# Gated cross-attention in fp32 on one core: probabilities transposed once per batch, their stacked rows copied by DMA inside SBUF, and the loads around the value loop reordered

## The chip, the core and the metric

The kernel runs on one core of a Trainium2 chip. The metric is the device time in microseconds (us) of the whole program.

## What is computed

With x of 16 x 512 x 512 (batch, queries, width) and a context of 16 x 77 x 512:

```
qp = x @ Wq + bq;  kp = ctx @ Wk + bk;  vp = ctx @ Wv + bv
w  = softmax(qp @ kp^T / sqrt(512))            # 512 x 77 for each batch
a  = w @ vp
gate = concat(qp, a) @ Wg + bg
out  = a * mask * sigmoid(gate) + x
```

## The kernel before, in words

Everything is fp32 in and out. Matmuls run on operands split into a high part (rounded to the matmul's own type, fp32r) and a low part (what the rounding leaves); a product is the sum of high x high, high x low and low x high.

**Set-up.** The program first makes weight products: `g`, `wqg` (the first half of the gate as a matrix applied to x), and `mt` (the keys folded with Wq and Wk). Then the value loop runs over ten tiles of 128 context rows (`k` = 0 to 9, plus one closing round). Each round transposes the values of the tile before (`turn_v`), makes the next tile's values (`v`) and the gate's share of the values (`vg`). ScalarE (ACT) writes the high parts, VectorE (DVE) or GpSimd (POOL) the low parts, and SyncE's queue (SP) stores them to `v_dram` (`store_v`, `store_vg`). Into the last rounds SP mixes the loads of batch 0: `x_raw` (x transposed, four chunks; one buffer only) and `x_rows`. ScalarE and GpSimd split `x_raw` of batch 0 into `xT` (high L478, low L731) in round 7, between the pieces of the value loop.

**Batch loop.** For each of 16 batches TensorE runs, in this written order: `gate_main` for query tile 0 (12 matmuls, L414), half of `gate_main` for tile 1, `turn_probs` (eight transposes), the other half, `attend` 0 (four matmuls: two into the gate's bank, L437 and L438, two into the attention's bank, L444 and L445), `gate_main` 2, `attend` 1, the scores of the next batch (`scores_T`, 12 matmuls), `attend` 2, `gate_main` 3 with the transposes of the next scores (`turn_scores`, L383) in its middle, `attend` 3.

**Probabilities before.** The softmax is on VectorE, its exponential on ScalarE. The result `prob` is split into high and low. Attention needs high x v_high, low x v_high and high x v_low, which is three products of 77 rows each. They are packed into two matmuls: `w_a` holds the 77 high columns and 45 of them again, `w_b` the 77 low columns and the other 32 high ones. ScalarE makes the repeated columns (`stack_probs`, L537 and L538). TensorE transposes `w_a` and `w_b` (L424, L427), and ScalarE copies both results to `wT` (L559, L561). `v_ext`, loaded from `v_dram` by four DMAs (77, 77, 45 and 32 rows of 4 KB), stacks the values' high and low rows to match.

**Queues.** SP issues its transfers in program order, waits included: in a batch `v_ext` of the next batch, then a wait for all low parts of the next `xT` (`xT_lo`), `x_raw` of the batch after it, then four output stores, each followed by a load of `x_rows`. ScalarE's first `tanh` of the batch loop waits until every value store has landed, since its buffer lies where the stores read from.

Of the kernel before, what the change touches and what calls it, by code (L numbers as in the profile page):

```python
# [27 lines left out]
LO_A = 45  # L28
LO_B = S - LO_A
K_A, K_B = S + LO_A, S + LO_B  # L30
# [44 lines left out]
def build(nc, io):  # L75
    with ExitStack() as es:
# [29 lines left out]
        w_a = sb("w_a", D0 + 6272, [P, T, K_A])  # L106
        w_b = sb("w_b", D0 + 6784, [P, T, K_B])
# [38 lines left out]
        prob = shifted  # L146
# [56 lines left out]
        def _(sync):  # L203
# [71 lines left out]
            for k in range(KT):  # L275
# [3 lines left out]
                if k == 5:  # L279
                    sync.wait_ge(dots_made, DOT["sb", 3] + 1)  # L280
                    load_xT(0, (0, 1))
                if k == 6:
                    load_xT(0, (2, 3))
                if k == 7:
# [3 lines left out]
                if k == 8:  # L288
# [29 lines left out]
        def _(pe):  # L318
# [57 lines left out]
            def turn_scores(b):  # L376
# [3 lines left out]
                else:  # L380
                    pe.wait_ge(wTb_made, b)
# [35 lines left out]
            def turn_probs(b):  # L417
                pe.wait_ge(prob_split, b + 1)
                pe.wait_ge(stacked_a, b + 1)
                pe.wait_ge(stacked_b, b + 1)  # L420
                if b == 0:
                    pe.wait_ge(job_drained, last_in_bank(7))
                for t in range(T):
                    last = pe.transpose(turn_ps[0:K_A, t * P:(t + 1) * P], w_a[:, t, :], ident[:, :])  # L424
                last.then_inc(wa_turned, 1)
                for t in range(T):
                    last = pe.transpose(score_ps[0:K_B, t * P:(t + 1) * P], w_b[:, t, :], ident[:, :])  # L427
                last.then_inc(wb_turned, 1)

            def attend(b, t):  # L430
                n, q, v = b * T + t, slice(t * P, (t + 1) * P), v_ext[b % 2]
                if t == 0:
                    pe.wait_ge(wTa_made, b + 1)
                    pe.wait_ge(wTb_made, b + 1)
                    pe.wait_ge(vext_in[b % 2], 64 * (b // 2 + 1))
                ps = gate_ps[n % 3]
                pe.matmul(ps[:, :], wT[0:K_A, 0, q], v[0:K_A, 0, D:2 * D], start=False, stop=False)  # L437
# [6 lines left out]
                pe.matmul(ps[:, :], wT[0:K_A, 0, q], v[0:K_A, 0, 0:D], start=True, stop=False)  # L444
# [22 lines left out]
        def _(act):  # L467
# [67 lines left out]
            def stack_probs(b):  # L535
                act.wait_ge(prob_hi, b + 1)
                act.activation(w_a[:, :, S:K_A], w_a[:, :, 0:LO_A], ACT.Copy).then_inc(stacked_a, 1)  # L537
                act.activation(w_b[:, :, S:K_B], w_a[:, :, LO_A:S], ACT.Copy).then_inc(stacked_b, 1)  # L538
# [256 lines left out]
```

## Time and profile before

| what | value |
|---|---|
| time, median of 3 runs | 432.78 us (431.98 to 433.77) |
| time of the profiled execution | 434.12 us |
| its span | 432.3 us |
| TensorE busy | 417.7 us (97%) |
| VectorE, ScalarE, GpSimd busy | 215.5, 151.9, 126.8 us |
| mean granted TensorE clock | 0.992 of full |
| DMA | 90.86 MB, mean 210 GB/s |

A busy TensorE is not one at its peak: its matmuls are pipelined and each row's duration holds the overlap with its neighbours, so lengths of stretches are read from start times. In the chain of work the durations run from one step to the next and add up to the span.

### The profile page before, as it was taken

To read this page: it belongs to the slowest core of one execution; us is meant where nothing else is said; L and a number is where in the kernel's file an instruction comes from. 1 tells how busy PE (TensorE), PEld (TensorE's weight loads), DVE (VectorE), ACT (ScalarE), POOL (GpSimd) and SP (SyncE) were. 2 spreads that over 40 slices of the span, in tenths; PEclk is the share of its full clock that TensorE was granted. 3 is DMA by queue.
4 is the path that set the end of the run, shared out by engine and by line. 5 is a ranking of instruction groups with operands and counts; after the bars stand their busy time and mean duration, and the time that the engine had idled before them with its cause. 6 is when DMAs were issued, how large, how long until landed. Compare 5 with 4: busy or idle time off the path is not lost.

```text
span 432.3 us, 5334 instructions
## 1 busy us (share of the span) xinstructions
PE 417.7 (97%) x1940; PEld 335.3 (78%) x1940; DVE 215.5 (50%) x385; ACT 151.9 (35%) x283; POOL 126.8 (29%) x98
## 2 busy tenths in 40 slices
PE   8999999998996999999999999999999999999996
PEld 4879978886774787787877878787787878778784
DVE  4786546553450646354463634546253553725453
ACT  5644243224222243241423324143342424324131
POOL 0004154346524051340505225050432505143100
PEclk9999999999898999999999999999999999999999
DMA  8975434457589766957577595766758567685312
GB/s 271 389 276 213 143 83 192 155 205 226 195 243 265 249 182 228 291 158 259 187 229 237 182 278 167 240 199 231 226 198 277 162 230 211 216 253 194 119 49 97
DMA packets 43125, 90.86 MB, mean 210 GB/s; under 512 B 5276, under 2 KB 5276, under 8 KB 42460
## 3 DMA queue, kind: packets, MB, share of 16 engines
q1 hardware_dynamic: 42524, 89.48, 63.5%
q10 hardware_dynamic: 576, 1.05, 0.6%
q8 instruction: 15, 0.25, 0.2%
q14 instruction: 10, 0.08, 0.1%
HBM read 63.51 MB, written 27.00 MB: 209 GB/s over the span
## 4 chain that ended last, share of the span: by engine, by line
PE 90%; DMA 5%; DVE 2%; ACT 1%; POOL 1%; SPq 1%; issue 0%; DVEq 0%; ACTq 0%
PE bank L414 40%; PE bank L322 31%; PE bank L437 4%; PE bank L438 4%; PE bank L444 3%; PE bank L445 3%; DMA v_ext<-v_dram 2%; PE bank L424 2%; PE bank L427 2%; DMA x_raw<-in_xT 1%; DMA wqT_raw<-in_wqT 1%; PE bank L383 1%; PE bank L365 1%; DMA v_dram<-v_st 1%; POOL v_st L731 1%
## 5 line engine op out<-in xcount | busy, mean ns | idle before, releaser
L414 PE MATMUL bank<-wqg,xT 128*128 128x512 f32 x768 | 191.8, 396 | 0.0
L414 PEld LDWEIGHTS bank<-wqg,xT 128*128 128x128 f32 x768 | 142.8, 189 | 29.4
L731 POOL TENSOR_TENSOR xT<-x_raw,xT 128x512 fp32r<-128x512 f32 x64 | 87.9, 1403 | 191.3 <-ACT xT L478 191.3
L695 DVE SCALAR_TENSOR_TENSOR prod_sb<-tanh_sb,bank 128x512 f32<-128x512 f32 x64 | 43.9, 686 | 123.1 <-ACT tanh_sb L550 123.1
L550 ACT ACTIVATE tanh_sb<-bank 128x512 f32<-128x512 f32 x64 | 38.4, 599 | 129.3 <-PE bank L438 121.7
L706 DVE SCALAR_TENSOR_TENSOR out_sb<-prod_sb,half_mask,x_rows 128x512 f32<-128x512 f32 x64 | 49.1, 768 | 1.7
L322 PE MATMUL bank<-xT,mt 128*77 128x512 f32 x192 | 47.1, 394 | 0.0
L322 PEld LDWEIGHTS bank<-xT,mt 128*77 128x77 f32 x192 | 28.0, 146 | 15.7
L478 ACT ACTIVATE xT<-x_raw 128x512 fp32r<-128x512 f32 x64 | 35.2, 617 | 3.2 <-DMA x_raw<-in_xT 3.2
L322 PE MATMUL bank<-wg,vT 128*128 128x512 f32 (+1 forms) x120 | 30.7, 407 | 2.6 <-DVE vT L577 2.6
L322 PE MATMUL bank<-wv,ctxT 128*128 128x512 f32 (+1 forms) x120 | 30.2, 401 | 0.0
L322 PEld LDWEIGHTS bank<-wg,vT 128*128 128x128 f32 (+1 forms) x120 | 23.3, 195 | 8.7 <-DVE vT L577 3.0
L437 PE MATMUL bank<-v_ext,wT 122*128 122x512 f32 x64 | 25.7, 402 | 4.2 <-DMA v_ext<-v_dram 4.2
L322 PE MATMUL bank<-ctxT,g_s 128*128 128x416 f32 x144 | 27.4, 352 | 0.6 <-DVE ctxT L573 0.6
L322 PEld LDWEIGHTS bank<-ctxT,g_s 128*128 128x128 f32 x144 | 26.8, 188 | 1.3 <-DVE ctxT L573 1.0
L444 PE MATMUL bank<-v_ext,wT 122*128 122x512 f32 x64 | 25.8, 403 | 0.0
L438 PE MATMUL bank<-v_ext,wT 109*128 109x512 f32 x64 | 25.7, 402 | 0.0
L445 PE MATMUL bank<-v_ext,wT 109*128 109x512 f32 x64 | 25.7, 402 | 0.0
L322 PEld LDWEIGHTS bank<-wv,ctxT 128*128 128x128 f32 (+1 forms) x120 | 21.7, 186 | 4.6
L533 ACT ACTIVATE expd<-shifted 128x308 f32<-128x308 f32 x16 | 7.4, 462 | 38.6 <-DVE shifted L675 38.6
L592 DVE TENSOR_SCALAR sT<-bank,sb_c 77x512 f32<-77x512 f32 x16 | 12.0, 747 | 17.8 <-PE bank L322 17.8
L731 POOL TENSOR_TENSOR v_st<-vg_f,v_st 128x512 fp32r<-128x512 f32 (+1 forms) x10 | 13.4, 1338 | 16.5 <-ACT v_st L469 16.5
(75 smaller groups left out, 378.7 us busy)
## 6 DMA issues: line engine op xcount, KB each, us to landing
x_raw<-in_xT SPq DMA_DIRECT2D x64, 256.0 KB, 5.2
x_rows<-in_x SPq DMA_DIRECT2D x64, 256.0 KB, 3.7
out_y<-out_sb SPq DMA_DIRECT2D x64, 256.0 KB, 2.0
v_ext<-v_dram SPq DMA_DIRECT2D x32, 308.0 KB
v_dram<-v_st SPq DMA_DIRECT2D x18, 512.0 KB, 3.2
v_ext<-v_dram SPq DMA_DIRECT2D x16, 180.0 KB
ctxT_raw<-in_ctxT SPq DMA_DIRECT2D x4, 624.0 KB, 10.7
ctx_rows<-in_ctx SPq DMA_DIRECT2D x4, 616.0 KB
```

The lines of the kernel that those rows point to most:

```text
L322: last = pe.matmul(ps, lhs(s, c), rhs(m, c), start=(c == 0 and n == 0), stop=(c == C - 1 and n == 2))
L414: pe.matmul(gate_ps[n % 3][:, :], xT[b % 2][:, s, c, q], wqg[:, m, c, :], start=(c == 0 and (s, m) == PRODUCTS[0]), stop=False)
L437: pe.matmul(ps[:, :], wT[0:K_A, 0, q], v[0:K_A, 0, D:2 * D], start=False, stop=False)
L438: pe.matmul(ps[:, :], wT[0:K_B, 1, q], v[0:K_B, 1, D:2 * D], start=False, stop=True).then_inc(gate_done, 1)
L444: pe.matmul(ps[:, :], wT[0:K_A, 0, q], v[0:K_A, 0, 0:D], start=True, stop=False)
L445: pe.matmul(ps[:, :], wT[0:K_B, 1, q], v[0:K_B, 1, 0:D], start=False, stop=True).then_inc(attn_done, 1)
L478: act.activation(xT[b % 2][:, HI, c], x_raw[:, c], ACT.Copy).then_inc(xT_hi, 1)
L550: act.activation(tanh_sb[:, n % 2, :], gate_ps[n % 3][:, :], ACT.Tanh, scale=0.5).then_inc(tanh_made, 1)
L592: dve.tensor_scalar(sT[:, :], sT_ps[0:S, :], sb_c[:, b:b + 1], None, ALU.add).then_inc(sT_made, 1)
L695: dve.scalar_tensor_tensor(prod_sb[:, n % 2, :], tanh_sb[:, n % 2, :], 1.0, attn_ps[n % 2][:, :], ALU.add, ALU.mult).then_inc(prod_made, 1)
L706: dve.scalar_tensor_tensor(out_sb[:, t, :], prod_sb[:, n % 2, :], half_mask[:, n:n + 1], x_rows[b % 2][:, t, :], ALU.mult, ALU.add).then_i ...
L731: pool.tensor_tensor(dst, src, f32(hi_), ALU.subtract).then_inc(made, 1)
```

## The change

The probabilities are no longer split before the transposes. VectorE writes them in fp32 with 19 of the 77 columns repeated (96 in all). TensorE transposes them once (four transposes in place of eight), ScalarE copies the 96 rows to `wT` as the high part, VectorE subtracts this from the transposed fp32 values to give the low part (`low_probs`), and two DMAs issued by ScalarE copy 2 x 32 high rows to partitions 96 to 127 of `wT`'s two halves. The transposes stand after the first `gate_main`; all of the second stands behind them. `attend` 0 waits for both copies and for the low part. `v_ext` takes five loads, one of them of 19 rows. The split of the next batch's `xT` by ScalarE follows the copy to `wT` and the two DMA issues. In the value loop the loads of `x_raw` and `x_rows` for batch 0 are issued one round earlier, and `v_ext` of batch 0 goes ahead of `x_raw` of batch 1.

```diff
-LO_A = 45
-LO_B = S - LO_A
-K_A, K_B = S + LO_A, S + LO_B
+Q = 32
+TOP = 3 * Q
+DUP = S - (TOP - S)
+K_B = TOP + DUP - Q
...
-                sync.dma_start(f32(v_ext[i][S:K_A, 0, :]), v_dram[r:r + LO_A, LO, :]).then_inc(vext_in[i], 16)
-                sync.dma_start(f32(v_ext[i][S:K_B, 1, :]), v_dram[r + LO_A:r + S, LO, :]).then_inc(vext_in[i], 16)
+                sync.dma_start(f32(v_ext[i][S:TOP, 0, :]), v_dram[r + DUP:r + S, LO, :]).then_inc(vext_in[i], 16)
+                sync.dma_start(f32(v_ext[i][TOP:P, 0, :]), v_dram[r:r + Q, LO, :]).then_inc(vext_in[i], 16)
+                sync.dma_start(f32(v_ext[i][S:K_B, 1, :]), v_dram[r + DUP - (K_B - S):r + DUP, LO, :]).then_inc(vext_in[i], 16)
...
-                if k == 5:
+                if k == 4:
                     sync.wait_ge(dots_made, DOT["sb", 3] + 1)
                     load_xT(0, (0, 1))
+                if k == 5:
+                    load_xT(0, (2, 3))
...
-            sync.wait_ge(xT_lo, C)
-            load_xT(1)
             sync.wait_ge(job_done, J["v", KT - 1] + 1)
             wait_stored(2)
             load_vext(0)
+            sync.wait_ge(xT_lo, C)
+            load_xT(1)
             load_vext(1)
...
-                    pe.wait_ge(wTb_made, b)
+                    pe.wait_ge(shift_made, b)
...
-                pe.wait_ge(prob_split, b + 1)
-                pe.wait_ge(stacked_a, b + 1)
-                pe.wait_ge(stacked_b, b + 1)
+                pe.wait_ge(prob_made, b + 1)
+                pe.wait_ge(prob_twice, b + 1)
...
-                    last = pe.transpose(turn_ps[0:K_A, t * P:(t + 1) * P], w_a[:, t, :], ident[:, :])
-                last.then_inc(wa_turned, 1)
-                for t in range(T):
-                    last = pe.transpose(score_ps[0:K_B, t * P:(t + 1) * P], w_b[:, t, :], ident[:, :])
-                last.then_inc(wb_turned, 1)
+                    last = pe.transpose(turn_ps[0:TOP, t * P:(t + 1) * P], prob[:, t, :], ident[:, :])
+                last.then_inc(turned, 1)
...
-                    pe.wait_ge(wTa_made, b + 1)
-                    pe.wait_ge(wTb_made, b + 1)
-                    pe.wait_ge(vext_in[b % 2], 64 * (b // 2 + 1))
+                    pe.wait_ge(wT_dup, 32 * (b + 1))
+                    pe.wait_ge(wT_lo, b + 1)
+                    pe.wait_ge(vext_in[b % 2], 80 * (b // 2 + 1))
...
+            def high_probs(b):
+                act.wait_ge(turned, b + 1)
...
+                act.activation(wT[0:TOP, 0, :], turn_ps[0:TOP, :], ACT.Copy).then_inc(wT_top, 1)
+                act.wait_ge(wT_top, b + 1)
+                act.dma_start(f32(wT[TOP:P, 0, :]), f32(wT[0:Q, 0, :])).then_inc(wT_dup, 16)
+                act.dma_start(f32(wT[TOP:P, 1, :]), f32(wT[Q:2 * Q, 0, :])).then_inc(wT_dup, 16)
...
-                stack_probs(b)
+                high_probs(b)
                 if more:
                     xT_hi_of(b + 1)
-                act.wait_ge(wa_turned, b + 1)
-                act.activation(wT[0:K_A, 0, :], turn_ps[0:K_A, :], ACT.Copy).then_inc(wTa_made, 1)
-                act.wait_ge(wb_turned, b + 1)
-                act.activation(wT[0:K_B, 1, :], score_ps[0:K_B, :], ACT.Copy).then_inc(wTb_made, 1)
...
+            def low_probs(b):
+                dve.wait_ge(wT_top, b + 1)
+                dve.tensor_tensor(wT[0:S, 1, :], turn_ps[0:S, :], f32(wT[0:S, 0, :]), ALU.subtract).then_inc(wT_lo, 1)
```

TensorE at the start of a batch, before the change. L414 is `gate_main`, L424 and L427 are the transposes, L437 to L445 are `attend`; `wqg`, `xT` and `wT` are named above.

```order
L414 MATMUL bank<-wqg,xT_69 128x512 x18
L424 MATMUL bank<-ident,w_a 122x128 x4
L427 MATMUL bank<-ident,w_b 109x128 x4
L414 MATMUL bank<-wqg,xT_69 128x512 x6
L437 MATMUL bank<-v_ext_60,wT 128x512
```

The same place after the change, where the lines have moved by one or two:

```order
L415 MATMUL bank<-wqg,xT_68 128x512 x12
L426 MATMUL bank<-ident,prob 96x128 x4
L415 MATMUL bank<-wqg,xT_68 128x512 x12
L436 MATMUL bank<-v_ext_60,wT 128x512
```

Four transposes are gone, the others stand six matmuls earlier, and twelve matmuls in place of six lie between them and `attend`.

ScalarE in one batch, before: the two stacking copies, the high parts of the next `xT`, the two copies to `wT`, the tanhs.

```order
L537 ACTIVATE w_a<-w_a 128x4x45
L538 ACTIVATE w_b<-w_a 128x4x32
L478 ACTIVATE xT_70<-x_raw 128x512 x4
L559 ACTIVATE wT<-bank 122x512
L561 ACTIVATE wT<-bank 109x512
L550 ACTIVATE tanh_sb<-bank 128x512 x3
```

And after:

```order
L539 ACTIVATE wT<-bank 96x512
L541 DMA wT<-wT 32x512
L542 DMA wT<-wT 32x512
L476 ACTIVATE xT_69<-x_raw 128x512 x4
L554 ACTIVATE tanh_sb<-bank 128x512 x3
```

The copy to `wT` and two DMA issues now stand ahead of the `xT` split, which stood ahead of the copies to `wT`.

SP at the end of the value loop, before (L261 is `store_vg`, L256 `store_v`, L251 the loads of `x_raw`, L265 to L268 those of `v_ext`; the last L261 is the last value store):

```order
L256 DMA v_dram<-v_st_75 192x1x512
L261 DMA v_dram<-v_st_74 256x1x512
L251 DMA x_raw<-in_xT 128x512 x4
L265 DMA v_ext_60<-v_dram 77x1024
L266 DMA v_ext_60<-v_dram 77x1024
L267 DMA v_ext_60<-v_dram 45x1024
L268 DMA v_ext_60<-v_dram 32x1024
L265 DMA v_ext_61<-v_dram 77x1024
```

And after, down to the last value store:

```order
L265 DMA v_ext_60<-v_dram 77x1024
L266 DMA v_ext_60<-v_dram 77x1024
L267 DMA v_ext_60<-v_dram 19x1024
L268 DMA v_ext_60<-v_dram 32x1024
L269 DMA v_ext_60<-v_dram 45x1024
L251 DMA x_raw<-in_xT 128x512 x4
L265 DMA v_ext_61<-v_dram 77x1024
L266 DMA v_ext_61<-v_dram 77x1024
L267 DMA v_ext_61<-v_dram 19x1024
L268 DMA v_ext_61<-v_dram 32x1024
L269 DMA v_ext_61<-v_dram 45x1024
L261 DMA v_dram<-v_st_74 192x1x512
```

`v_ext` of batch 0 now goes first, with a load of 19 rows in it, and `x_raw` of batch 1 stands between the two `v_ext`.

## Rows read from the trace of the kernel before

**Rows 1.** The page: engines' busy time, and shares of the chain that ended last.

```profile
PE 417.7 (97%) x1940; PEld 335.3 (78%) x1940; DVE 215.5 (50%) x385; ACT 151.9 (35%) x283; POOL 126.8 (29%) x98
PE 90%; DMA 5%; DVE 2%; ACT 1%; POOL 1%; SPq 1%; issue 0%; DVEq 0%; ACTq 0%
```

**Rows 2.** TensorE's waits: releaser, total us, times, longest us.

```profile
PE bank L437 <- DMA v_ext<-v_dram: 4.2, 1, 4.2
PE bank L322 <- DVE vT L577: 2.6, 1, 2.6
```

**Rows 3.** The chain in order of time: start us, length us, step.

```profile
85.43 5.53 PE bank L322 x24
91.39 5.54 PE bank L322 x24
101.01 5.19 DMA x_raw<-in_xT
108.73 4.57 PE bank L322 x12
113.74 5.54 PE bank L322 x24
...
126.70 9.58 DMA v_ext<-v_dram
138.47 3.40 PE bank L414 x12
```

**Rows 4.** The chain in the batch that starts at 225 us.

```profile
225.39 4.10 PE bank L414 x18
229.48 0.44 PE bank L424 x4
...
232.69 2.74 PE bank L414 x12
...
236.37 2.79 PE bank L322 x12
```

**Rows 5.** Timeline of that batch: start us, length us, engine, instruction, idle before.

```profile
226.69 2.18 ACT L478 ACTIVATE xT<-x_raw 128x512 fp32r<-128x512 f32 x4
227.39 5.57 POOL L731 TENSOR_TENSOR xT<-x_raw,xT 128x512 fp32r<-128x512 f32 x4 [13.12 <-ACT xT L478]
228.98 0.41 SPq L265 DMA_DIRECT2D v_ext<-v_dram  x1
229.32 0.60 PE L424 MATMUL bank<-ident,w_a 128*122 128x128 f32 x4
229.96 0.60 ACT L559 ACTIVATE wT<-bank 122x512 fp32r<-122x512 f32 x1 [1.08 <-PE bank L424]
```

**Rows 6.** Windows: busy us, then granted clock, DMA share, GB/s at the end.

```profile
229.00:229.50 0.50, 0.50 (x5) 0.37 (x4) 0.00 (x0) 0.00 (x0) 0.50 (x2) 1.00 1.00 389
231.50:232.00 0.50, 0.50 (x4) 0.42 (x3) 0.00 (x0) 0.00 (x0) 0.50 (x2) 1.00 0.68 246
...
136.40:140.00 3.60, 3.58 (x9) 2.88 (x10) 0.00 (x0) 0.00 (x0) 0.00 (x0) 0.54 0.76 261
```

**Rows 7.** Issue time (ns, min/median/max) and landing: wkT_raw's (two rows), out_y's.

```profile
L481 ACTq DMA_DIRECT2D wkT_raw<-in_wkT x4: 404/456/627, 0.7 to 2.1; - x4
DMA to landing us min/median/max: 3.6/5.6/7.7
...
DMA to landing us min/median/max: 2.0/2.0/6.8
```

**Rows 8.** Timeline of batch 0.

```profile
129.63 0.60 SPq L261 DMA_DIRECT2D v_dram<-v_st  x1
140.59 0.60 ACT L550 ACTIVATE tanh_sb<-bank 128x512 f32<-128x512 f32 x1 [7.56 <-DMA v_dram<-v_st]
141.23 0.69 DVE L695 SCALAR_TENSOR_TENSOR prod_sb<-tanh_sb,bank 128x512 f32<-128x512 f32 x1 [11.76 <-ACT tanh_sb L550]
147.74 0.43 PE L383 MATMUL bank<-ident,sT 77*128 77x77 f32 x4
```

More of the change, by code:

```diff
@@ L105, in build @@
         expd = sb("expd", D0 + 5952, [P, T, S])
[L106 to L107 removed]
+        prob = sb("prob", D0 + 6272, [P, T, TOP])
         wv = sb("wv", E0, [P, 2, C, D], F32R)
@@ L417, in turn_probs @@
             def turn_probs(b):
[L418 to L420 removed]
+                pe.wait_ge(prob_made, b + 1)
+                pe.wait_ge(prob_twice, b + 1)
                 if b == 0:
                     pe.wait_ge(job_drained, last_in_bank(7))
+                else:
+                    pe.wait_ge(wT_lo, b)
                 for t in range(T):
[L424 to L428 removed]
+                    last = pe.transpose(turn_ps[0:TOP, t * P:(t + 1) * P], prob[:, t, :], ident[:, :])
+                last.then_inc(turned, 1)
             def attend(b, t):
@@ L432, in attend @@
                 if t == 0:
-                    pe.wait_ge(wTa_made, b + 1)
-                    pe.wait_ge(wTb_made, b + 1)
-                    pe.wait_ge(vext_in[b % 2], 64 * (b // 2 + 1))
+                    pe.wait_ge(wT_dup, 32 * (b + 1))
+                    pe.wait_ge(wT_lo, b + 1)
+                    pe.wait_ge(vext_in[b % 2], 80 * (b // 2 + 1))
                 ps = gate_ps[n % 3]
-                pe.matmul(ps[:, :], wT[0:K_A, 0, q], v[0:K_A, 0, D:2 * D], start=False, stop=False)
+                pe.matmul(ps[:, :], wT[:, 0, q], v[:, 0, D:2 * D], start=False, stop=False)
                 pe.matmul(ps[:, :], wT[0:K_B, 1, q], v[0:K_B, 1, D:2 * D], start=False, stop=True).then_inc(gate_done, 1)
@@ L443, in attend @@
                 ps = attn_ps[n % 2]
-                pe.matmul(ps[:, :], wT[0:K_A, 0, q], v[0:K_A, 0, 0:D], start=True, stop=False)
+                pe.matmul(ps[:, :], wT[:, 0, q], v[:, 0, 0:D], start=True, stop=False)
                 pe.matmul(ps[:, :], wT[0:K_B, 1, q], v[0:K_B, 1, 0:D], start=False, stop=True).then_inc(attn_done, 1)
@@ L450, in _ @@
                 gate_main(b, 0)
-                gate_main(b, 1, range(0, C // 2))
                 turn_probs(b)
-                gate_main(b, 1, range(C // 2, C))
+                gate_main(b, 1)
                 attend(b, 0)
@@ L533, in exps @@
                 act.activation(expd[:, :, :], shifted[:, :, :], ACT.Exp, scale=SCALE).then_inc(exp_made, 1)
[L535 to L538, printed above, removed]
+            def high_probs(b):
+                act.wait_ge(turned, b + 1)
+                if b == 0:
+                    act.wait_ge(wT_zeroed, 1)
+                else:
+                    act.wait_ge(attn_done, b * T)
+                act.activation(wT[0:TOP, 0, :], turn_ps[0:TOP, :], ACT.Copy).then_inc(wT_top, 1)
+                act.wait_ge(wT_top, b + 1)
+                act.dma_start(f32(wT[TOP:P, 0, :]), f32(wT[0:Q, 0, :])).then_inc(wT_dup, 16)
+                act.dma_start(f32(wT[TOP:P, 1, :]), f32(wT[Q:2 * Q, 0, :])).then_inc(wT_dup, 16)
             def tanh_tile(b, t):
@@ L707, in output @@
                                          x_rows[b % 2][:, t, :], ALU.mult, ALU.add).then_inc(out_made, 1)
+            dve.wait_ge(job_done, J["v", KT - 1] + 1)
+            dve.memset(f32(wT[2 * Q:TOP, 1, :]), 0.0).then_inc(wT_zeroed, 1)
             softmax_max(0)
             softmax_rest(0)
+            dve.wait_ge(wT_zeroed, 1)
             for b in range(B):
                 more = b + 1 < B
+                low_probs(b)
                 product(b, 0)
```

19 lines of the change are left out of this document (7 added, 12 removed).

## The prediction

> **What bounds the kernel now.** I read the page first: TensorE is busy 97% of the span, and 90% of the chain that ended last is TensorE [rows 1]. So in a batch only two things count: TensorE's own instructions, and any wait newly put in front of them. The list of TensorE's waits shows where it does not run: once 4.2 us for `v_ext` and once 2.6 us for `vT` [rows 2]. In the 15 batches behind the first it waits for nothing. The chain in order of time then says what these two waits cost in all. Rounds of the value loop start every 5.96 us (85.43, 91.39); three rounds after 91.39 would be 109.27, and the chain has that start at 113.74, so the wait behind the late `x_raw` (a step of 5.19 us from 101.01) costs 4.47 us, not 2.6. The rest is clock: the 12 matmuls behind the wait take 4.57 us [rows 3] where 12 like them take 2.79 [rows 4]. The same shows behind the 4.2 us wait, where the granted clock is 0.54 (near 1.2 GHz in place of 2.4 [rows 6]) and 12 gate matmuls take 3.40 us [rows 3] against 2.74 [rows 4]. Last I read the timeline of one batch for the distances between transposes, copies and the `xT` split [rows 5], and of batch 0 for what stands behind its wait [rows 8].
>
> **1. The earlier `x_raw` of batch 0.** ScalarE waits in round 7 for chunks that SP issued only just before, and the transposed values queue behind it. One round earlier is 5.96 us earlier, more than the 5.19 us of the transfer. The wait and its slow clock go: -4.47 us. ScalarE still does four more high parts in that round and GpSimd four low ones, so the next piece may be late by some tenths: I take -4.2, with -3.0 and -4.5 as bounds.
>
> **2. The start of batch 0.** `v_ext` of batch 0 no longer stands behind 1 MB of `x_raw`. Its transfer took 9.58 us from 126.70 [rows 3]; issued some 2.5 us earlier and ahead of that megabyte, it should cease to hold TensorE: -4.2, and about -1.6 more by the clock. But what is late next? ScalarE's first tanh began at 140.59, released by the last value store, which was issued at 129.63 [rows 8]. That store stays behind both `v_ext` and `x_raw`, so the tanh is not earlier relative to the loop. `attend` 2 needs its product (0.69 us [rows 8]) and the next transposes of scores (147.74 before) need VectorE behind two products and two outputs, which I put at 144.9 if the store lands as now. So this part gives at most -2.9, not -5.8.
> The store can also be later. Between 231.5 and 232 us, when only the 77-row loads of `v_ext` are moving, the DMA share is 0.68 at 246 GB/s, against 1.00 at 389 when 128-row transfers move [rows 6]: 0.68 is 11 of 16 engines, 22 GB/s each, and 77 is 7 x 11. If a load's rows are dealt only in equal parts, 19 rows (78 KB) go to one engine: 3.5 us for each of the two `v_ext` ahead of the store, +7 us if nothing else is waited for, and then the tanh costs +4 instead. I take the middle, a store later by 2.5 us: -0.5 in all, bounds -2.9 and +4.
> The page "DMA: Bandwidth & Descriptors" of the Trainium skill (section "Why a DMA increments its semaphore by 16 and not by 1") says that a DMA uses the largest number of engines up to 16 that divides the slowest dimension: 11 for 77 rows, 1 for 19. The trace agrees for the 77.
> Within later batches the 19 rows cost nothing: `v_ext` is issued at 228.98 [rows 5] for an `attend` a whole batch (18.7 us) later.
>
> **3. Four transposes fewer.** Each group of four takes 0.44 us of the chain [rows 4]. 15 batches x -0.44 = -6.6 us (batch 0's is hidden in part 2). ScalarE's stacking and VectorE's split lie beside TensorE's work and are worth nothing. The low part, new on VectorE (77 x 512 out of PSUM, as long as a product, 0.69), runs beside the DMA copies and ends before them. The probabilities are wanted six matmuls (1.4 us) earlier, and VectorE saves two steps ahead of that; only in batch 0 is TensorE likely to wait (about 0.9 us, inside part 2).
>
> **4. The new wait, the copies.** Count from the first transpose (T). ScalarE's copy begins at T+0.64 and takes 0.60 (229.96 against 229.32 [rows 5]), so the first copy's DMA can be issued at T+1.29. An issue on ScalarE takes at least 0.40 us [rows 7], so the second starts at T+1.69. TensorE has 0.44 of transposes and 2.74 of gate matmuls [rows 4], and loads the weights of `attend` about 0.2 earlier: it wants `wT` at T+2.99. What is not in the trace is the landing of a 64 KB copy inside SBUF. Nearest rows: `out_y`, 256 KB, lands at best 2.0 us after its issue; `wkT_raw`, also on ScalarE's queue and beside SP's loads, at best 3.6 [rows 7]. Less the time of the 192 KB more that `out_y` moves (0.5 us at 389 GB/s), the lower bound is 1.5: landed T+3.19, a wait of 0.2. At 3.6 the wait is 2.3. I take 2.0, smaller than `out_y` but in the midst of the `v_ext` and `x_rows` traffic: landed T+3.69, a wait of 0.7 us per batch, nearer the lower row since size and target are nearer to it. 15 x 0.7 = +10.5. The gap should be too short for the clock to fall.
>
> **5. The `xT` split.** It moves behind the copy and both issues. ScalarE starts it at T+2.1; GpSimd follows 0.70 later and takes 5.57 [rows 5]: done at T+8.4. TensorE, without part 4's wait, wants it for the next scores at T + 0.44 + 2.74 + 0.94 + 3.68 = T+7.8 (0.94 is `attend`: 3.68 from 232.69 to 236.37 less 2.74 [rows 4]). So even with instant copies it would wait some 0.56 us in 14 batches. Behind a wait of 0.7 this is covered and adds nothing, but it is a floor: at most 0.14 of part 4 could be won back by faster copies. SP's `x_raw` moves later by as much and has 12 us to spare.
>
> **Sum:** -4.2 - 0.5 - 6.6 + 10.5 = -0.8 us. On the profiled span that is 432.3 to 431.5. The profiled execution took 434.12, 1.8 more than its span and 1.3 above the median, and on the median of 432.78 the forecast is 432.0: no change. A measurement can tell about 0.5% (2.2 us) from none.
>
> **Rivals.**
> (a) Faster: the copies land in 1.5 us and the last value store as now. Then part 5's floor decides: 14 x 0.56 + 0.2 = +8.0, part 2 gives -2.9: -4.2 - 2.9 - 6.6 + 8.0 = -5.7, so 427.1. If the issues are shorter or GpSimd takes 4 x 1.3 alone, 424. For it: no wait at all today and light traffic at that moment in parts of a batch; against it: the 1.00 DMA share at 229 us [rows 6], just where the copies will run. Chance 0.32.
> (b) Slower: the copies queue behind the `v_ext` packets on each engine. At a landing of 2.7 the wait is 1.4, 15 x 1.4 = +21, sum +9.7: 442.5. It decides from a wait of 0.9 (a landing of 2.2) upward; at 3.6 the time would be 456. For it: the same busy share, and two queues that shared the engines at the start landed in 3.6 or later. Chance 0.28.
> The section "Queues, rings and completion order" of the same page of the Trainium skill says that an engine takes whole packets of many descriptors from one queue before it turns to the next; each `v_ext` load gives an engine seven rows of 4 KB, and behind those a copy would be late by about 1 us each. No row here shows it.
> (c) Slower by the first batch: the 19-row loads keep one engine behind, the first tanh is late by 6 us or more, part 2 is +4 and the clock falls once more (+1.8): 438. Chance 0.06.
> (d) The reorder does nothing, since the value loop waits for GpSimd's split instead: part 1 is 0, 436. Chance 0.03.
>
> **How the numbers follow.** The forecast (within 0.5%, 430.6 to 434.9) has 0.31. Range 426 to 443: it takes in (a)'s main value and (b)'s, and leaves out (a)'s 424 and (b)'s tail, together 2 in 10. The forecast's own range is 430 to 435. Faster 0.33 is (a) and the forecast's edge; slower 0.35 is (b), (c) and half of (d); same 0.32.
>
> **What would show it.** Part 1: no TensorE wait for `vT` near 106 us, and the batch loop starting some 4 us earlier, near 121. Part 2: no wait for `v_ext`, a wait for a product or for `sT` in batch 0. Part 3: one group of four transposes, 0.44 us. Part 4: 15 waits of `attend` 0 for DMA `wT`, 0.7 us each. Part 5: waits of the scores for GpSimd near zero. The prediction is wrong if the landing of the copies is not about 2.0 us, or if the clock falls behind each wait.

## The result, and the profile after

The changed kernel takes 550.59 us (median of 4 runs, 546.04 to 552.31) beside 433.27 us (431.98 to 434.62) for the kernel before on the same chip: 1.269 times as long, with a 95% interval of 1.260 to 1.278. The forecast was 432.0 with a range of 426 to 443.

The page after, busy time and the shares of the chain that ended last, to be held against [rows 1]:

```profile
PE 443.5 (82%) x1876; PEld 347.8 (64%) x1876; DVE 216.2 (40%) x386; ACT 136.7 (25%) x235; POOL 118.1 (22%) x98
PE 65%; DMA 23%; ACT 3%; DVE 2%; SPq 2%; POOL 2%; issue 2%; ACTq 1%; DVEq 0%
```

TensorE has 64 instructions fewer, as the change says, and yet is busy 26 us longer: each matmul takes longer on average, which is a slower clock (the profiled execution has a granted clock of 0.912 in the mean, before 0.992). And DMA, 5% of the chain before, is 23%. The list of TensorE's waits (total us, times, longest) names the transfer:

```profile
PE bank L436 <- DMA wT<-wT: 89.9, 16, 7.0
PE bank L426 <- DVE prob L685: 1.4, 1, 1.4
...
PE bank L323 <- DVE vT L577: 0.9, 1, 0.9
```

Sixteen waits for the copies of 64 KB inside SBUF. Fifteen of them are 6.0 us long in the mean ((89.9 - 0.5) / 15). The last batch loads no `v_ext` for a batch behind it, and there the second copy takes 2.00 us and the wait is 0.5 us. A row of the chain and one of TensorE's timeline:

```profile
528.01 2.00 DMA wT<-wT
```

```profile
530.06 0.50 PE L436 MATMUL bank<-v_ext,wT 128*128 128x512 f32 x1 [0.51 <-DMA wT<-wT]
```

The wait for `vT` fell from 2.6 to 0.9 and that for `v_ext` is gone [rows 2]. There is none for GpSimd's `xT`.

The chain after, in the batch that answers to [rows 4] (start us, length us, step):

```profile
233.59 0.45 PE bank L426 x4
...
234.06 0.60 ACT wT L539
...
234.69 0.54 ACTq L541
...
235.26 7.16 DMA wT<-wT
...
242.47 0.79 PE bank L436
243.26 0.43 PE bank L437
...
244.54 4.25 PE bank L415 x12
...
257.44 2.78 PE bank L415 x12
```

One group of four transposes is left, 0.45 us. Then come ScalarE's copy, the first issue, and 7.16 us of the second copy's transfer, under which TensorE's twelve gate matmuls lie. Behind the wait three of the four matmuls of `attend` take 0.43 us each (0.23 at 249 us), and the twelve gate matmuls 4.25 us (2.78 a little later, at 257.44): the clock is down. Between 155.94 and 501.48 us this chain has 14 steps `DMA wT<-wT`, one in each batch that loads `v_ext`, so a batch takes (501.48 - 155.94) / 13 = 26.6 us in place of 18.7.

The timeline of that batch, beside [rows 5]:

```profile
233.43 0.60 PE L426 MATMUL bank<-ident,prob 128*96 128x128 f32 x4
233.69 0.41 SPq L265 DMA_DIRECT2D v_ext<-v_dram  x1
234.06 0.60 ACT L539 ACTIVATE wT<-bank 96x512 fp32r<-96x512 f32 x1 [3.09 <-PE bank L426]
...
234.69 0.54 ACTq L541 DMA_DIRECT2D wT<-wT  x1
...
235.19 0.42 SPq L269 DMA_DIRECT2D v_ext<-v_dram  x1
235.26 0.61 ACTq L542 DMA_DIRECT2D wT<-wT  x1
242.47 0.79 PE L436 MATMUL bank<-v_ext,wT 128*128 128x512 f32 x1 [5.69 <-DMA wT<-wT]
```

SP issues its five loads of `v_ext`, nearly 1 MB, from 0.26 us behind the first transpose on. Both copies are issued in the midst of them, and they land last. The issues are nearly where the prediction put them (T+1.26 and T+1.83, T being 233.43, where it had T+1.29 and T+1.69). What is far off is the landing, the time from the issue until the last piece has arrived. The transfers issued in 0.1 us from 234.68 and from 235.25 (KB each, us from issue to landing) give it for either copy:

```profile
wT<-wT ACTq DMA_DIRECT2D x1, 64.0 KB, 5.8
...
wT<-wT ACTq DMA_DIRECT2D x1, 64.0 KB, 7.2
```

What moved meanwhile shows in the packets of the two queues (q1 is SP's, q10 ScalarE's; packets, MB, share of 16 engines) in 236.5 to 237.5, 237.5 to 239 and 239 to 240.5 us:

```profile
q1 hardware_dynamic: 47, 0.14, 53.4%
q10 hardware_dynamic: 22, 0.03, 8.7%
...
q1 hardware_dynamic: 99, 0.34, 65.3%
q10 hardware_dynamic: 10, 0.01, 2.2%
...
q1 hardware_dynamic: 65, 0.18, 43.2%
q10 hardware_dynamic: 50, 0.07, 16.0%
```

For 1.5 us the engines carry 99 packets of `v_ext` and 10 of the copies, then 50 of the copies in as long a time. The last 13 packets of the copies go in the 2 us behind these windows. The windows of that time (us, busy of PE, PEld, DVE, ACT and POOL, then clock, DMA share, GB/s) say what is still moving, and what TensorE gets:

```profile
237.50:238.50 1.00, 0.00 (x0) 0.00 (x0) 0.00 (x0) 0.61 (x2) 1.00 (x2) 1.00 0.67 223
...
240.50:242.50 2.00, 0.03 (x1) 0.03 (x1) 0.00 (x0) 0.00 (x0) 1.05 (x1) 0.58 0.10 35
...
241.50:242.00 0.50, 0.00 (x0) 0.00 (x0) 0.00 (x0) 0.00 (x0) 0.06 (x1) 0.50 0.06 25
...
243.00:247.50 4.50, 4.50 (x12) 3.47 (x11) 1.44 (x2) 0.60 (x1) 0.00 (x0) 0.50 0.81 270
```

First a share of 0.67, which is 11 of 16 engines as in [rows 6]. In the last two microseconds it is 0.10, and 0.06, one engine of 16, from 241.5 to 242 us. These rows don't name the load that is still moving. That it is the one of 19 rows fits e1 below, where these rows are split: there such a share (0.10) lasts only from 239.0 to 239.5 us ahead of the second copy's landing at 239.9. The granted clock, 1.00 while TensorE first stands, is 0.58 there and 0.50 (1.2 GHz in place of 2.4) in the 4.5 us behind the wait, though TensorE is busy all through them.

Batch 0, the timeline beside [rows 8]:

```profile
121.60 2.97 PE L415 MATMUL bank<-wqg,xT 128*128 128x512 f32 x12
126.00 0.61 PE L426 MATMUL bank<-ident,prob 128*96 128x128 f32 x4 [1.43 <-DVE prob L685]
128.39 0.59 SPq L261 DMA_DIRECT2D v_dram<-v_st  x1
135.73 0.79 PE L436 MATMUL bank<-v_ext,wT 128*128 128x512 f32 x1 [6.35 <-DMA wT<-wT]
144.49 1.09 ACT L554 ACTIVATE tanh_sb<-bank 128x512 f32<-128x512 f32 x2 [6.71 <-DMA v_dram<-v_st]
148.69 0.48 PE L384 MATMUL bank<-ident,sT 77*128 77x77 f32 x4
```

The batch loop starts at 121.60, 3.6 us earlier than before (125.21 there). At the next transposes of scores, 148.69 against 147.74, this and more is gone again.

**Where the time went.** The spans differ by 111.7 us. The waits for the copies are 89.9 of it. The loop's start gives -3.6, the transposes 16 x -0.44 = -7.0, the lost `v_ext` wait -4.2, the wait for `prob` +1.4. What is left, 111.7 - 89.9 + 3.6 + 7.0 + 4.2 - 1.4 = 35.2 us, is 2.3 us for each of the 15 long waits. That fits the slow clock. In the batch shown it is 4.25 - 2.77 for twelve gate matmuls and 2.08 - 0.94 for `attend`, 2.6 us together. Over the 14 batches of the chain the twelve matmuls behind the wait take 3.2 to 4.7 us, 3.96 in the mean, and with `attend` that is 2.3 us more than at full clock.

### The profile page after: what moved, and what is told of

The parts are those of the page before. It is cut to its first block, busy times and chain, and to the rows that moved or that the text cites. A ratio compares the mean times of both kernels' runs of the same rounds, so it can differ in the third digit from the quotient of the medians.

```text
span 544.0 us, 5238 instructions
## 1 busy us (share of the span) xinstructions
PE 443.5 (82%) x1876; PEld 347.8 (64%) x1876; DVE 216.2 (40%) x386; ACT 136.7 (25%) x235; POOL 118.1 (22%) x98
## 4 chain that ended last, share of the span: by engine, by line
PE 65%; DMA 23%; ACT 3%; DVE 2%; SPq 2%; POOL 2%; issue 2%; ACTq 1%; DVEq 0%
PE bank L415 26%; PE bank L323 23%; DMA wT<-wT 19%; PE bank L436 4%; PE bank L437 3%; PE bank L444 3%; PE bank L443 3%; DMA v_dram<-v_st 3%; ACT wT L539 2%; ACTq L541 1%; PE bank L426 1%; POOL xT L738 1%; PE bank L384 1%; DMA wkT_raw<-in_wkT 1%; POOL v_st L738 1%
## 5 line engine op out<-in xcount | busy, mean ns | idle before, releaser
L415 PE MATMUL bank<-wqg,xT 128*128 128x512 f32 x768 | 211.4, 425 | 0.0
L415 PEld LDWEIGHTS bank<-wqg,xT 128*128 128x128 f32 x768 | 158.4, 210 | 36.7
L738 POOL TENSOR_TENSOR xT<-x_raw,xT 128x512 fp32r<-128x512 f32 x64 | 79.5, 1273 | 309.3 <-ACT xT L476 309.3
L436 PE MATMUL bank<-v_ext,wT 128*128 128x512 f32 x64 | 31.2, 488 | 89.9 <-DMA wT<-wT 89.9
L436 PEld LDWEIGHTS bank<-v_ext,wT 128*128 128x128 f32 x64 | 13.5, 211 | 99.3 <-DMA wT<-wT 96.7
L323 PE MATMUL bank<-wg,vT 128*128 128x512 f32 (+1 forms) x120 | 29.1, 391 | 0.9 <-DVE vT L577 0.9
L444 PE MATMUL bank<-v_ext,wT 122*128 122x512 f32 x64 | 28.9, 452 | 0.0
L443 PE MATMUL bank<-v_ext,wT 128*128 128x512 f32 x64 | 28.9, 452 | 0.0
L437 PE MATMUL bank<-v_ext,wT 122*128 122x512 f32 x64 | 28.8, 450 | 0.0
L323 PEld LDWEIGHTS bank<-wg,vT 128*128 128x128 f32 (+1 forms) x120 | 22.1, 185 | 6.5 <-DVE vT L577 1.3
L690 DVE TENSOR_TENSOR wT<-bank,wT 77x512 fp32r<-77x512 f32 x16 | 11.0, 687 | 29.8 <-ACT wT L539 29.8
L539 ACT ACTIVATE wT<-bank 96x512 fp32r<-96x512 f32 x16 | 9.5, 596 | 48.3 <-PE bank L426 48.3
```

Source lines behind the costliest of these rows:

```text
L323: last = pe.matmul(ps, lhs(s, c), rhs(m, c), start=(c == 0 and n == 0), stop=(c == C - 1 and n == 2))
L415: pe.matmul(gate_ps[n % 3][:, :], xT[b % 2][:, s, c, q], wqg[:, m, c, :], start=(c == 0 and (s, m) == PRODUCTS[0]), stop=False)
L436: pe.matmul(ps[:, :], wT[:, 0, q], v[:, 0, D:2 * D], start=False, stop=False)
L437: pe.matmul(ps[:, :], wT[0:K_B, 1, q], v[0:K_B, 1, D:2 * D], start=False, stop=True).then_inc(gate_done, 1)
L443: pe.matmul(ps[:, :], wT[:, 0, q], v[:, 0, 0:D], start=True, stop=False)
L444: pe.matmul(ps[:, :], wT[0:K_B, 1, q], v[0:K_B, 1, 0:D], start=False, stop=True).then_inc(attn_done, 1)
```

## The experiments

Three theories stood at the start. A: the copies queue behind the loads of `v_ext` on each DMA engine (the prediction's rival (b)). B: a copy inside SBUF from ScalarE's queue takes that long by itself. C: the load of 19 rows, all on one engine, holds up the pieces of the copies there. All kernels start from the changed one unless said otherwise. The table sums them up; "wait" is TensorE's in total for the copies, and "landing" the median over both copies of all 16 batches.

| kernel | time, us | ratio to before (95%) | wait, us | landing, us |
|---|---|---|---|---|
| changed kernel | 550.59 | 1.269 (1.260 to 1.278) | 89.9 | 6.7 |
| e1_split19 | 539.47 | 1.244 (1.235 to 1.252) | 83.8 | 6.3 |
| e2_late_vext | 450.60 | 1.039 (1.033 to 1.046) | 23.9 | 2.4 |
| e3_engine_rows | 443.74 | 1.023 (1.016 to 1.030) | none | none |
| e4_reorder_only | 431.30 | 0.994 (0.991 to 0.997) | none | none |
| e5_vext_with_copies | 543.92 | 1.246 (1.237 to 1.256) | 85.2 | 5.2 |
| e6_one_load_early | 459.69 | 1.057 (1.052 to 1.063) | 30.9 | 2.9 |
| e7_xT_first | 423.14 | 0.973 (0.968 to 0.977) | none | none |
| e8_xraw_earlier_only | 431.28 | 0.992 (0.989 to 0.994) | none | none |
| e9_together_split19 | 523.77 | 1.205 (1.197 to 1.213) | 72.6 | 4.8 |
| e10_small_shares | 472.07 | 1.086 (1.079 to 1.094) | 39.2 | 3.6 |
| e11_xT_first_19rows | 428.86 | 0.987 (0.982 to 0.993) | none | none |
| e12_dma_late_xT_first | 440.10 | 1.015 (1.008 to 1.022) | 14.2 | 2.2 |

The kernel before had medians of 433.82, 434.61 and 434.49 us beside the first, second and third four.

### e1_split19: the 19 rows as 16 and 3

```diff
-                sync.dma_start(f32(v_ext[i][S:TOP, 0, :]), v_dram[r + DUP:r + S, LO, :]).then_inc(vext_in[i], 16)
+                sync.dma_start(f32(v_ext[i][S:S + 16, 0, :]), v_dram[r + DUP:r + DUP + 16, LO, :]).then_inc(vext_in[i], 16)
+                sync.dma_start(f32(v_ext[i][S + 16:TOP, 0, :]), v_dram[r + DUP + 16:r + S, LO, :]).then_inc(vext_in[i], 16)
...
-                    pe.wait_ge(vext_in[b % 2], 80 * (b // 2 + 1))
+                    pe.wait_ge(vext_in[b % 2], 96 * (b // 2 + 1))
```

> The changed kernel with the 19-row load of v_ext issued as two, of 16 and of 3 rows; all else the same. In the changed kernel the two wT copies land 7.0 us after their issue, and in the last 1.5 us before that only one DMA engine is busy (share 0.06 to 0.08). Theory A (the copies wait on each engine for the v_ext rows that SP queued ahead of them, the engine that has all 19 rows being the last): the tail of one engine goes, landing near 5 us, the wait of attend 0 falls from 5.6 to about 3.5 us, the kernel from 550 to some 505 to 515 us. Theory B (a copy inside SBUF takes some 7 us whatever else moves): no change, 550 us. Theory C (the 19 rows on one engine are the whole cause): landing 2 to 2.5 us, about 440 us.

539.47 us. The waits are 6.1 us less in all (83.8 against 89.9), the time 11. The copies land in 6.3 us in place of 6.7. The 19-row load is not what holds them, and C falls as the main cause. A is not hit either: more is left than it said.

### e2_late_vext: the loads of `v_ext` behind the first `attend`

```diff
-                    sync.wait_ge(attn_done, b * T)
+                    sync.wait_ge(attn_done, b * T + 1)
                     load_vext(b + 1)
```

> The changed kernel with v_ext of the next batch issued after attend 0 of the running batch in place of before it, so that only an x_rows load is near the copies. Theory A: the copies land in 2 to 2.5 us, the wait of attend 0 is under 1 us in all batches but the first, the clock stays up, about 435 to 445 us. Theory B: landing stays near 7 us, about 550 us. Theory C: as A, since the 19-row load is moved too.

One constant takes 100 us off: 450.60. Here are the two copies of the batch at 232 us, each from a view of what is issued in 0.1 us or less (KB, us to landing), and then the windows from 235 us (columns as above):

```profile
wT<-wT ACTq DMA_DIRECT2D x1, 64.0 KB, 2.3
...
wT<-wT ACTq DMA_DIRECT2D x1, 64.0 KB, 3.2
```

```profile
235.00:236.50 1.50, 0.00 (x0) 0.00 (x0) 0.00 (x0) 1.11 (x3) 1.50 (x2) 1.00 0.05 18
236.50:239.00 2.50, 2.49 (x11) 2.05 (x12) 1.05 (x2) 0.60 (x1) 2.50 (x3) 1.00 0.07 16
```

The same copies with the same issues land in 2.4 us (median). So B falls: without the loads a copy is quick, as the last batch of the changed kernel already said. What made it slow is the loads of `v_ext` beside it. And behind a gap of 1.5 us the granted clock stays at 1.00. Of the 23.9 us of waits 6.2 is batch 0, where the loads are where they were; the other 15 wait 1.2 us each in the mean, from 0.5 to 2.0, and behind none of them does the clock fall.

### e3_engine_rows: the copies by ScalarE itself

```diff
-                act.dma_start(f32(wT[TOP:P, 0, :]), f32(wT[0:Q, 0, :])).then_inc(wT_dup, 16)
-                act.dma_start(f32(wT[TOP:P, 1, :]), f32(wT[Q:2 * Q, 0, :])).then_inc(wT_dup, 16)
+                act.activation(wT[TOP:P, 0, :], f32(wT[0:Q, 0, :]), ACT.Copy).then_inc(wT_dup, 1)
+                act.activation(wT[TOP:P, 1, :], f32(wT[Q:2 * Q, 0, :]), ACT.Copy).then_inc(wT_dup, 1)
```

TensorE waits for `2 * (b + 1)` of them, and ahead of the transposes for those of the batch before.

> The changed kernel with the 2 x 32 rows copied inside SBUF by two ScalarE activations (0.6 us each) in place of two DMAs. By all theories the wait for a DMA goes. ScalarE is then done at T+2.4 (T is the first transpose), before TensorE wants wT at T+3.0; the xT split starts at T+2.4 and GpSimd ends near T+8.4, so the scores wait about 0.5 us in 14 batches. Sum against the kernel before: -3.6 for the earlier batch loop, +1 to +4 for the later first tanh, -7.0 for 64 transposes, +7 for the scores' wait: 430 to 436 us. If instead something else of the change costs the time, it stays well above 440.

443.74 us, above what was expected. TensorE's waits, and below them ScalarE's first copy among the instructions on `wT` (ns, min/median/max):

```profile
PE bank L323 <- POOL xT L739: 13.3, 15, 1.8
...
PE bank L437 <- DMA v_ext<-v_dram: 2.3, 1, 2.3
```

```profile
L542 ACT ACTIVATE wT<-wT x16: 628/628/630, 127.3 to 425.7; 32x512 fp32r<-32x512 f32 x16
```

Each copy takes ScalarE 0.63 us, about what an issue of the DMA took (0.54 and 0.61), and it is finished then. No wait for `wT` is left. In its place stands the one that the prediction's part 5 had as a floor: the scores wait for GpSimd's `xT`, 1.8 us in batch 0 and 0.82 us in each of 14 others (0.56 was worked out), since the split stands behind the copies on ScalarE.

### e4_reorder_only: the kernel before with both reorders of loads

The edit is the two hunks of the change on `k == 5` to `k == 8` and on `load_xT(1)`, alone, in the kernel before.

> The kernel before with the reordered loads alone: x_raw and x_rows of batch 0 a round earlier, v_ext of batch 0 ahead of x_raw of batch 1. The probabilities and the four v_ext loads (77, 77, 45, 32 rows) are as before. Expected: the wait for vT falls from 2.6 to 0.9 us and the batch loop starts 3.6 us earlier; without 19-row loads the first tanh starts no later than before (140.6), and the v_ext wait of 4.2 us goes. 425 to 429 us. If the later first tanh (144.5 in the changed kernel) came from the order of the loads and not from the 19 rows, it shows here too and the time is 429 to 432.

431.30 us, a gain of 2.5 and less than expected. A row from its waits and one from its timeline:

```profile
PE bank L437 <- ACT wT L559: 4.5, 1, 4.5
```

```profile
137.11 0.60 ACT L550 ACTIVATE tanh_sb<-bank 128x512 f32<-128x512 f32 x1 [3.94 <-DMA v_dram<-v_st]
```

The `vT` wait is down to 0.9 us as in the changed kernel. `v_ext` is in time now, but `attend` waits 4.5 us for ScalarE's `wT`: this copy stands in order behind the split of `x_raw` of batch 1, which `v_ext` has pushed back. One wait took the place of the other. And the first tanh is at 137.11, where the changed kernel, with the same reorders and the 19-row loads, has it at 144.49.

### e5_vext_with_copies: loads and copies issued together

Since C and B had fallen and A had the size wrong, the question was what the engines do when both queues have work. If they served in the order of arrival (A1), it should help to release the loads not ahead of the copies but with them:

```diff
-                    sync.wait_ge(attn_done, b * T)
+                    sync.wait_ge(wT_top, b + 1)
                     load_vext(b + 1)
```

> The changed kernel with the five v_ext loads released by the copy to wT (the same event that releases the wT copies) in place of some 1 us before it, so that both queues are filled together. Runs so far: v_ext issued first, landing 6.7 us in the median; v_ext after attend 0, 2.4 us; 19 rows split, 6.3 us. Theory A1 (an engine takes work of both queues in order of arrival): only the v_ext load or two issued by then stand ahead, landing 3 to 4.5 us, kernel 465 to 500 us. Theory A2 (the engines favour SP's queue, or take turns with many rows at a time, as long as SP's has work): landing stays at 6 to 7 us, 535 to 555 us.

543.92 us: next to nothing. The two copies of the batch at 235 us, as for e2:

```profile
wT<-wT ACTq DMA_DIRECT2D x1, 64.0 KB, 3.4
...
wT<-wT ACTq DMA_DIRECT2D x1, 64.0 KB, 7.3
```

The first lands 2.4 us sooner than in the changed kernel, but the second, issued 0.5 us later, when only two loads had been issued, lands as late as behind all five. By the order of arrival it would stand behind two loads, 14 rows on an engine or 2.6 us at 22 GB/s [rows 6]. This run alone leaves one way out: if the load of 19 rows, issued 0.2 us behind the copy, got ahead of it, one engine would have 33 rows to move, some 6 us. e9 below closes it: with these rows split the second copies still take 6.3 us in the median of the 14 batches. So it is not the order of arrival, and A1 falls.

### e6_one_load_early: one of the five loads ahead of the copies

```diff
                     sync.wait_ge(attn_done, b * T)
-                    load_vext(b + 1)
+                    load_vext_first(b + 1)
+                    sync.wait_ge(attn_done, b * T + 1)
+                    load_vext(b + 1, False)
```

`load_vext_first` is the load of line 265 (77 rows), and the other call the four others.

> A dose: the changed kernel with one 77-row load of v_ext (308 KB on 11 engines) issued ahead of the copies as now, the other four after attend 0. If the copies wait for what is queued ahead of them, the landing lies between 2.4 us (none ahead) and 6.7 us (all ahead), by about the 1.2 us that 28 KB take on an engine: 3.5 to 4 us, kernel 465 to 485 us. If a small amount of traffic is enough to hold them, it stays above 5 us and 510 us.

459.69 us, waits of 30.9 us. In the 14 batches that load `v_ext` the mean wait is 1.22 us in e2, 1.68 here and 5.93 in the changed kernel. So one load of 77 rows ahead costs 0.5 us a batch and all five cost 4.7: ten times as much for three times the bytes. Behind two of these 14 waits, all of 1.4 to 1.9 us, the granted clock did fall (0.50 near 200 and 364 us), and these batches took 22.0 and 22.1 us where the others took 20.0 to 20.5.

### e7_xT_first: ScalarE's copies, with the split of `xT` ahead

e3 and e1 together, and in ScalarE's batch:

```diff
+                if more and b:
+                    xT_hi_of(b + 1)
                 high_probs(b)
-                if more:
+                if more and not b:
                     xT_hi_of(b + 1)
```

> The run with ScalarE copies in place of the DMAs took 443.7 us, with the scores waiting for GpSimd's xT split 15 times, 0.88 us each. Here ScalarE's high parts of the next xT are moved ahead of the copy to wT (from batch 1 on) and the 19-row load is issued as 16 and 3 rows. The split then starts 2 us earlier and ends before the scores want it; ScalarE is free again at T-0.3, before the transposes are done. Expected: no wait in batches 1 to 15, a batch of 18.3 us in place of 18.7: 443.7 - 13 for the waits - 2 for the first tanh = 426 to 430 us. If the order of ScalarE is not what costs the 0.88 us, it stays near 443.

423.14 us: 2.7% faster than the kernel before (0.968 to 0.977), and a little better than expected. Its waits in the batch loop are all in batch 0, 4.0 us together. The two longest:

```profile
PE bank L428 <- DVE prob L689: 1.4, 1, 1.4
PE bank L445 <- DVE prod_sb L702: 1.2, 1, 1.2
```

Of the 11.5 us that it gains, 3.3 are the earlier `x_raw` (e8 below). The 14 middle batches take 18.33 us in place of 18.71, together 5.3 us, which fits the four transposes fewer. The rest is in batch 0.

### e8_xraw_earlier_only: the kernel before with the first reorder alone

The edit is the hunk on `k == 5` to `k == 8`.

> The kernel before with x_raw and x_rows of batch 0 a round earlier and nothing else (v_ext of batch 0 stays behind x_raw of batch 1). The run with both reorders took 431.3 against 433.8 us. If the earlier x_raw is what gains, this one begins its batch loop 3.6 us earlier as well and keeps the 4.2 us wait for v_ext: 429 to 431 us. If both reorders were needed, 433 us.

431.28 us, a gain of 3.3. The wait for `v_ext` is still 4.2 us. So the first reorder gives all of e4's gain, and `v_ext` ahead of `x_raw` adds nothing to the kernel before that these runs can tell.

### e9_together_split19 and e10_small_shares: by what pieces do the engines take turns?

Two readings were left. T: an engine turns to the other queue only when it is through with a load's whole share of rows on it (7 of 4 KB for a 77-row load, 19 for the other), so a copy, which has pieces on all 16 engines, waits for shares of that size. S: SP's queue goes ahead as long as it has any work. e9 is e5 and e1 together. e10 leaves the time of the loads as it was and cuts them into shares of 1 to 3 rows:

```diff
-                sync.dma_start(f32(v_ext[i][0:S, 0, :]), v_dram[r:r + S, HI, :]).then_inc(vext_in[i], 16)
-                sync.dma_start(f32(v_ext[i][0:S, 1, :]), v_dram[r:r + S, HI, :]).then_inc(vext_in[i], 16)
...
+                for s in range(2):
+                    for p0, p1 in ((0, 32), (32, 64), (64, S)):
+                        sync.dma_start(f32(v_ext[i][p0:p1, s, :]), v_dram[r + p0:r + p1, HI, :]).then_inc(vext_in[i], 16)
+                for p0, p1 in ((S, S + 16), (S + 16, TOP)):
+                    sync.dma_start(f32(v_ext[i][p0:p1, 0, :]), v_dram[r + DUP + p0 - S:r + DUP + p1 - S, LO, :]).then_inc(vext_in[i], 16)
```

> Both queues filled together, as in the run where the copy to wT releases v_ext, and the 19-row load issued as 16 and 3 rows. In that run the first copy landed 3.4 us after its issue and the second 7.3, with 543.9 us. Theory T (an engine changes queue only after a DMA's whole share, so a copy waits for at most one share each time, and the second copy's last part waited for the 19-row share): no share is over 28 KB now, the second copy lands near 5 us, 490 to 515 us. Theory S (the engines serve SP's queue first while it has work): the second copy stays at 6.5 to 7.3 us, 530 to 545 us.

> The changed kernel with the same bytes of v_ext in the same place, but each 77-row load issued as 32, 32 and 13 rows and the 19 rows as 16 and 3: ten loads, and no engine has more than 3 rows (12 KB) of one, where it had 7 or 19. Theory T: a copy waits for shares of 8 to 12 KB, the second lands in 3 to 4 us, 455 to 480 us. Theory S: as much work of SP's is still there, landing 5 to 7 us, 510 to 545 us.

e9: 523.77 us, between the two, with copies at 3.3 and 6.4 us. e10: 472.07 us. The same megabyte, started at the same place, costs 78 us less. Its copies in the batch at 238 us:

```profile
wT<-wT ACTq DMA_DIRECT2D x1, 64.0 KB, 3.4
...
wT<-wT ACTq DMA_DIRECT2D x1, 64.0 KB, 3.8
```

S falls: from 241.0 to 242.5 us the engines move 91 packets of the copies beside 111 of `v_ext`. That the size of the shares matters is what T said, but e10 doesn't show it alone: ten issues take SP longer (the first six, 2.85 us), so that fewer of the loads are ahead of the copies. And e9's second copy is later than T allows. That the copies wait for `v_ext` on the engines is shown. The exact rule by which an engine changes queues stays open.

### e11_xT_first_19rows and e12_dma_late_xT_first: what each part is worth

e11 is e7 with the 19-row load as in the change. e12 is e7 with DMAs for the copies again, but with the loads of `v_ext` behind the first `attend` as in e2.

> The run of 423.1 us (ScalarE copies, xT split first, 19 rows issued as 16 and 3) without the last: the 19-row load as one. If the order on ScalarE is what took 443.7 to 423.1, the batches are 18.3 us long here too and only batch 0 is longer, by a first tanh some 4 to 7 us later of which 3 to 6 us reach TensorE: 426 to 429 us. If the split of the 19 rows counted in every batch, it is near 440.

> The changed kernel with its two wT copies by DMA, but with all that the runs showed to be in their way moved: v_ext after attend 0, xT split ahead of the copy to wT, 19 rows as 16 and 3. The copies should land in about 2.4 to 3.2 us, attend 0 waits about 1.2 us a batch. Against the 450.6 us with v_ext late alone: GpSimd's split no longer follows, the first batch gains some 4 us: 438 to 445 us, still slower than the kernel before and some 17 us behind the version with ScalarE copies. If it came below 430 the DMA itself would be no loss.

e11: 428.86 us. So the load of 19 rows costs 5.7 us (428.86 - 423.14), and the place of the split 14.9 (443.74 - 428.86). The first is all in batch 0, where `attend` waits for `v_ext`:

```profile
PE bank L437 <- DMA v_ext<-v_dram: 3.2, 1, 3.2
```

e12: 440.10 us, 5.6 us above the kernel before. Even with no `v_ext` load in their way but in batch 0, the version with DMA copies is 17 us slower than e7, the one with ScalarE's own. Its 14 middle batches take 0.8 us more each (19.14 against 18.33), and 5.2 us of its waits are in batch 0:

```profile
PE bank L437 <- DMA wT<-wT: 14.2, 16, 5.2
```

## Why the prediction was wrong

**The step that failed is in part 4**: "I take 2.0, smaller than `out_y` but in the midst of the `v_ext` and `x_rows` traffic", with an upper bound of 3.6. The copies landed 5.8 and 7.2 us behind their issues in the batch shown, 6.7 in the median. The time 2.0 was right for a copy without the loads beside it: 1.9 and 2.0 in the last batch of the changed kernel, a median of 2.2 in e12. Then the rest of the arithmetic holds too: e12's fifteen later waits are (14.2 - 5.2) / 15 = 0.6 us, where 0.7 was forecast. What was wrong is the choice "nearer the lower row since size and target are nearer to it". What decides is not what is copied but what else is queued, and [rows 7] had the row for this: `wkT_raw`, on ScalarE's queue beside SP's loads, took 3.6/5.6/7.7. Its minimum was taken as a bound, where its median and maximum were the case at hand. [Rows 5] had the other half: `v_ext` is issued 0.34 us ahead of the transposes, so nearly 1 MB starts just before the copies in 14 of the 16 batches. At the 22 GB/s of one engine [rows 6] the two times 7 rows of 4 KB on each of 11 engines are an estimated 2.6 us alone. That would have turned the forecast, though the copies were later still, by 4.3 us in the median (6.7 against 2.4 in e2). What makes up the rest is not shown.

**"The gap should be too short for the clock to fall"** followed from the 0.7 and fell with it. Behind the wait shown the clock was 0.50, and the slow stretches cost some 2.3 us for each of 15 long waits: 35 us that the sum had at zero. At e12's gaps of 0.5 to 0.7 us it didn't fall, so the sentence was right for the wait that it spoke of.

**Rival (b)** had the mechanism, and e2 shows it: queueing behind `v_ext`, with a chance of 0.28 and a price of 442.5 us, at most 456. Its price stopped at the same wrong bound. The sentence beside it drew on the Trainium skill, page "DMA: Bandwidth & Descriptors", section "Queues, rings and completion order": an engine drains a whole packet, typically 9 to 17 descriptors, from one queue before it turns to another. The trace agrees in its direction: 99 packets of `v_ext` to 10 of the copies for 1.5 us, then 50 of the copies. It doesn't show the size of a turn. By the prediction's "late by about 1 us each", the two loads of 77 rows would have given a landing of some 4 us and a wait of 2.7. This was there, but not carried into the price, and it too would have been short of the 6.7 measured.

**Part 1**, the earlier `x_raw`: -4.2 forecast. The loop starts 3.6 us earlier, and e8 is 3.3 us faster. Right, inside its bounds.

**Part 2**, the start of batch 0: -0.5 forecast, bounds -2.9 and +4. The reorder is worth nothing or slightly less than nothing (e4 against e8). The 19 rows on one engine are real: a DMA share of 0.10 at the end of the copies' wait, and 5.7 us in e11 against e7. With them the first tanh comes at 144.49, that is 22.9 us behind the start of the batch loop, where it was 15.4 before (140.59 [rows 8] less 125.21): 7.5 us later, as the upper bound supposed with its +7. The next transposes of scores are 4.6 us later by the same measure (27.1 against 22.5), where that bound had +4; but this holds batch 0's wait for the copies too. The same page of the Trainium skill, in its section "Why a DMA increments its semaphore by 16 and not by 1", gives a rule by which 19 rows go to one engine, and the share of 0.06 in the changed kernel's trace agrees. But the next thing late behind the old wait was not named: in e4 it is ScalarE's `wT`, stuck behind the split of batch 1.

**Part 3**, the transposes: 0.44 us a batch forecast, 0.45 of the chain left for the one group that stays. The middle batches of e7 and e11, in which TensorE waits for nothing, are 0.38 us shorter than before (18.33 against 18.71). Right in the main.

**Part 5**, the `xT` split: a floor of 0.56 us a batch, covered by the copies' wait. It is covered in the changed kernel (no wait for GpSimd), and bare in e3, where it is 0.82 us. The mechanism is right, and the size too small by a third: the two copies of e3 take ScalarE longer than the two issues were put at (1.31 us against 0.80), and the split starts at T+2.57 in place of T+2.1. The issues themselves were put too short: in the changed kernel they take 0.54 and 0.61 us, not 0.40.

**Rival (a)**, faster, supposed a landing of 1.5 us; the copies are never below 1.9. (c) was right about the 19 rows: it priced them at 6.3 us beside the forecast (4 + 0.5 + 1.8), and e11 against e7 measures 5.7. In the changed kernel this was small beside the copies' waits. (d) is refuted by the loop's start.

## What to carry to other kernels

Price a small transfer on the critical path by what is queued on the same DMA engines when it is issued, not by its size or by the best landing of its kind: the same 64 KB took 6.7 us or 2.4 in the median, by whether 1 MB of loads on another queue started 1 us before the first copy (233.69 against 234.69) or 5 us behind it (237.75 against 232.72 in e2). Where an engine can make the copy in the time of the issues (here 0.63 us each), it should, and what stood behind on this engine should go ahead of it: these two edits, with the 19-row load split, turn 1.27 times the time of before into 0.973. And when a sum gives TensorE a wait, put the slow clock behind it in the sum as a term, with the row of a wait of that length beside it.

## What the runs showed of the hardware

- A DMA of 32 rows of 2 KB inside SBUF, issued by ScalarE, lands in 1.9 us at best; its issue takes ScalarE 0.51 to 0.61 us in the median, more than the 0.40 taken from [rows 7].
- In the median over all batches, one 77-row load issued ahead of it on SP's queue made it 0.5 us later (2.4 to 2.9), all five 4.3 us later (6.7), ten smaller ones with the same bytes 1.2 (3.6).
- With a load of 19 rows of 4 KB among those of `v_ext`, one or two engines were still busy for 2 us when the others were done (a share of 0.10, and 0.06 in one half microsecond of it). The same rows as 16 and 3 took 11 us off the changed kernel and 5.7 off e11.
- TensorE's granted clock was 1.00 in the first microseconds of a wait, 0.58 in the last two of the wait shown, and 0.50 for 4.5 us of full work behind it. The gaps of 0.5 to 2.0 us in batches 1 to 15 of e2 left it at 1.00, while in e6 two gaps of 1.9 us were followed by a clock of 0.50. So the length of the gap alone doesn't decide.
- ScalarE copies 32 x 512 fp32 from partitions 0 to 31 to partitions 96 to 127 in 0.63 us.
